# x + h made on VectorE from x with two factors per row, in place of a sum on GpSimd

## The reference, cut to what matters

```
h       = layernorm(x)                       # per row: (x - mean) * rstd
normed  = rmsnorm(h) * norm_w
h_tilde = softmax(normed q k ...) @ [normed; context]
alpha   = sigmoid(h @ gate_w.T + gate_b)
x2      = x + (1 - alpha) * h + alpha * h_tilde
        = (x + h) + alpha * (h_tilde - h)
out     = x2 + experts(layernorm(x2))
```

## Time and profile before

| What | Value |
|---|---|
| median of 3 runs | 297.89 us |
| profiled execution, its own time | 297.96 us |
| its span, first to last instruction | 296.2 us |
| attention, pairs 0 to 7 | about 16 to 88 us of the span |
| PE busy | 264.8 us (89%) |
| DVE busy | 228.5 us (77%) |
| ACT busy | 176.5 us (60%) |
| POOL busy | 158.9 us (54%) |
| mean granted TensorE clock | 0.968 |

### The profile page before, as it was taken

How to read it: one execution, slowest core, us unless ns; L and a number is a source line. 1 busy time by engine, 2 the same in 40 slices (tenths; PEclk the granted TensorE clock), 3 DMA queues, 4 the chain that set the end, 5 groups by cost and what they waited for, 6 DMA issues and landing times.

```text
span 296.2 us, 5382 instructions
## 1 busy us (share of the span) xinstructions
PE 264.8 (89%) x1677; PEld 234.0 (79%) x1677; DVE 228.5 (77%) x534; ACT 176.5 (60%) x338; POOL 158.9 (54%) x150
## 2 busy tenths in 40 slices
PE   6559999998826999999999999999999999999960
PEld 2449879896722798999999898999999999989960
DVE  3698999999881499797797787797887887966341
ACT  2437699786633667648557666657566666745410
POOL 3446845566456741466566565646645645416605
PEclk9999999999985999999999999999999999999976
DMA  6995237454352674544644543554445441201201
GB/s 206 208 364 144 71 107 212 142 161 138 114 184 82 216 256 139 144 138 158 196 137 126 176 173 124 160 163 164 143 133 197 144 140 48 71 2 63 63 11 64
DMA packets 29137, 42.06 MB, mean 142 GB/s; under 512 B 5249, under 2 KB 22859, under 8 KB 28992
## 3 DMA queue, kind: packets, MB, share of 16 engines
q1 hardware_dynamic: 24512, 29.61, 32.6%
q0 software_dynamic: 4608, 12.24, 13.1%
HBM read 33.93 MB, written 8.45 MB: 143 GB/s over the span
## 4 chain that ended last, share of the span: by engine, by line
PE 70%; DVE 8%; issue 8%; POOL 5%; DMA 4%; ACT 2%; DVEq 0%; ACTq 0%; POOLq 0%
PE bank L1060 18%; PE bank L1061 18%; PE bank L1062 18%; PE bank L1132 4%; PE bank L1101 3%; POOL out_dram L507 2%; PE bank L1147 2%; POOL x_all L501 1%; PE bank L1168 1%; PE bank L1172 1%; PE bank L1169 1%; DVE hn_cnat L721 1%; PE bank L1121 1%; DVE setup_or_probs L816 1%; DMA x_all<-token_rows,idx_all 1%
## 5 line engine op out<-in xcount | busy, mean ns | idle before, releaser
L663 ACT ACTIVATE keysT<-bank,biasT 128x512 f32<-128x512 f32 (+1 forms) x65 | 43.9, 675 | 65.2 <-PE bank L1062 56.1
L507 POOL DMA_INDIRECT out_dram<-h,sidx x32 | 38.4, 1200 | 46.6 <-DVE h L950 39.3
L501 POOL DMA_INDIRECT x_all<-out_dram,idx_all x32 | 38.7, 1211 | 23.8 <-DMA out_dram<-h,sidx 16.2
L1060 PE MATMUL bank<-x_hi,w_hi 128*128 128x512 f32 (+1 forms) x114 | 45.2, 396 | 0.0
L1061 PE MATMUL bank<-x_lo,w_hi 128*128 128x512 f32 (+1 forms) x114 | 44.5, 390 | 0.0
L1062 PE MATMUL bank<-x_hi,w_lo 128*128 128x512 f32 (+1 forms) x114 | 44.0, 386 | 0.0
L497 POOL DMA_INDIRECT x_all<-token_rows,idx_all x28 | 27.4, 980 | 22.1 <-DVE factor L1006 15.4
L958 DVE SCALAR_TENSOR_TENSOR junk<-idx_rows,idx_f,normed 128x512 bf16<-128x512 bf16 (+1 forms) x32 | 38.9, 1215 | 0.0
L989 DVE TENSOR_TENSOR w_lo<-w_raw,w_hi 128x512 fp32r<-128x512 f32 x56 | 38.3, 684 | 0.1
L1062 PE MATMUL bank<-w_hi,g_lo 128*128 128x256 f32 x128 | 36.2, 283 | 0.0
L1060 PE MATMUL bank<-w_hi,g_hi 128*128 128x256 f32 x128 | 36.1, 282 | 0.1
(11 more groups left out here) (141 smaller groups left out, 711.9 us busy)
## 6 DMA issues: line engine op xcount, KB each, us to landing
w_raw<-in_L_ffn_W_dram SPq DMA_DIRECT2D x32, 512.0 KB, 3.7
hn_cnat<-in_ctx_dram SPq DMA_DIRECT2D x8, 256.0 KB, 2.7
idx_rows<-in_L_ffn_top_idx_dram SPq DMA_DIRECT2D x8, 256.0 KB, 4.0
out_dram<-x SPq DMA_DIRECT2D x8, 256.0 KB, 2.4
token_rows<-xn SPq DMA_DIRECT2D x7, 256.0 KB, 2.2
x_all<-in_x_dram SPq DMA_DIRECT2D x2, 768.0 KB, 11.2
hn_cnat<-in_L_ffn_b_dram SPq DMA_DIRECT2D x1, 1024.0 KB, 6.7
x_all<-in_x_dram SPq DMA_DIRECT2D x2, 256.0 KB, 3.7
```

Of the source, the lines that this page charges most:

```text
L501: g.indirect_dma_start(accg[:, t, :], None, flat, list_of(e, t)).then_inc(acc_in, 16)
L507: g.indirect_dma_start(flat, idx(sidx[:, t:t + 1].bitcast(U32), 0), newrow[:, t, :], None, bounds_check=N - 1, oob_is_err=False).then_inc( ...
L663: a.activation(g32[:, f % NG, c], ps_up[j % 2][:, c], ACT.Gelu_apprx_tanh, bias=bias)
L1060: t_.matmul(dst, lhs_hi, rhs_hi, start=first, stop=False)
```

## The change

POOL no longer computes x + h. DVE makes two factors per row once for all batches (in three groups, behind the statistics they come from) and then, in each pair, two `tensor_scalar` instructions of 256 numbers a row that multiply x by the one and add the other. They stand behind `h_rows` and ahead of the reciprocal and `shift`. `h_rows` no longer waits for POOL's reading of h, and `residual` waits for DVE's own instructions instead of POOL's.

```diff
+        xh_scale = sb("xh_scale", [P, NB])
+        xh_shift = sb("xh_shift", [P, NB])
...
             def attention(p, s, use):                      # POOL
-                pool.wait_ge(h_rdy, 2 * p + 2)
-                g.tensor_tensor(x_plus_h[:, s, :], x_all[:, ds(p * (2 * H), 2 * H)],
-                                h[:, s, :, :].rearrange("p b h -> p (b h)"), ALU.add).then_inc(xh_rdy, 1)
...
             def h_rows(p, s, reused=True):                 # DVE
                 if reused:
-                    dve.wait_ge(xh_rdy, p - 1)
                     dve.wait_ge(diff_rdy, 2 * p - 2)
...
+            def xh_factors(b0, b1_):
+
+                v.tensor_scalar(xh_scale[:, b0:b1_], pow_out[:, 0, b0:b1_], 1.0, None, ALU.add).then_inc(x_steps, 1)
+                v.tensor_tensor(xh_shift[:, b0:b1_], neg_mean[:, b0:b1_], pow_out[:, 0, b0:b1_], ALU.mult)\
+                    .then_inc(x_steps, 1)
+                steps[0] += 2
+
+            def x_plus_h_rows(p, s):
+
+                for b in range(2):
+                    v.tensor_scalar(x_plus_h[:, s, b * H:(b + 1) * H], x_all[:, ds((2 * p + b) * H, H)],
+                                    xh_scale[:, ds(2 * p + b, 1)], xh_shift[:, ds(2 * p + b, 1)],
+                                    ALU.mult, ALU.add).then_inc(xh_rdy, 1)
...
             def residual(p, s, use):
                 dve.wait_ge(mix_rdy, p + 1)
-                dve.wait_ge(xh_rdy, p + 1)
+                dve.wait_ge(xh_rdy, 2 * p + 2)
...
             def attention(p, s, use):                      # DVE
...
                     x_rms(10, NB, 5)
+                    xh_factors(10, NB)
...
                 if is_first(p):
                     x_variances(10, NB)
+                    xh_factors(0, 4)
+                    dve.wait_ge(x_steps, steps[0])
                 else:
                     aggr2(p - 1, 1 - s)
                     if not is_last(p):
                         h_rows(p + 1, 1 - s)
+                x_plus_h_rows(p, s)
                 dve.wait_ge(exp_rdy, 2 * p + 2)
                 v.reciprocal(rinv[:, :], rsum[:, :]).then_inc(ri_rdy, 1)
                 if is_first(p):
                     x_rms(4, 10, 4)
+                    xh_factors(4, 10)
                     dve.wait_ge(x_steps, steps[0])
...
-            dve.wait_ge(xh_rdy, NPAIR)
+            dve.wait_ge(xh_rdy, 2 * NPAIR)
```

## The result

The kernel after takes 305.43 us (305.39 to 307.19) against 297.76 us for the kernel before in the same runs: a ratio of 1.0267, with a 95% interval of 1.0224 to 1.0311. That is +7.7 us, where +10.0 us (308.0 us) was forecast; the time lies in the range and the mechanism is the one called the double block. The profiled execution took 305.46 us.

What follows compares the result with a forecast made beforehand. A loop through DVE, ACT and PE bounds the attention: 6.50 us from `shift`'s end to the next `h_rows`. 8.7 + 0.9 + 0.5 + 0 - 0.1 = +10.0 us, 297.96 + 10.0 = 308.0 us; range 300.0 to 309.5 us.

Steps and rivals of the forecast that it cites:

- the double block: Attention pairs 1 to 4: POOL's `w_lo` and `normed` each hold up DVE ahead of `shift`; 308.0 us, chance 0.50.
- (a): POOL drops its sum, 1.28 us a pair; `mix` and `residual` fall to 0.69 us, 0.7 to 0.9 us a pair.
- (b): Two new DVE rows a pair, ahead of the reciprocal and `shift`: 0.335 us each, 0.67 us for two.
- (c): New rows and `shift` wait for POOL's `w_lo` and `normed`; `shift` ends 3.75 or 3.85 us after H, start of `h_rows`.
- (d): Five attention beats, each from one `h_rows` start to the next: 50.07 against 41.37 us, +8.7 us.
- the single block: Rival in the attention beats: `w_lo` comes after the second row, only `shift` waits; beat 9.05 us, 303.2 us, chance 0.17.
- (e): Last pairs: pair 6 +0.9 us, `shift` waiting for `w_lo`; pair 7 +0.5 us, no POOL work beside it.
- (f): Pair 0: small instructions, a wait and two rows, 1.1 to 1.4 us, covered by DVE's waits: 0, other end +0.3 us.
- (g): Start: L721's second row is free 0.9 us earlier, but a load of x comes late next: -0.1 us.
- (h): Dropped or moved waits of `h_rows` and `residual`: cost 0; the experts move as a block.
- the sliding of `w_lo` behind `shift`: Rival in the attention: rows and `shift` finish before POOL's `w_lo` and `normed`; beat 8.0 us, 297.3 us, chance 0.15.
- No block for the new rows: Rival in the attention: POOL does not hold up the rows, `shift` waits for `w_lo` alone; 300.5 us, chance 0.13.

Runs made afterwards that it cites:

- two waits: Kernel after with POOL's `expert0_lo` waiting for `shift` and `normed_rows` waiting for `residual` of the same pair: ratio 0.9972 to the kernel before.
- The first of these waits: POOL's `expert0_lo` waits for `shift` of the same pair, here added to the kernel before: 299.08 us, ratio 1.0031.
- The kernel with the last rows early: Kernel after with the new rows ahead of `hnT_low`, those of pairs 6 and 7 one pair earlier: 299.31 us, ratio 1.0027.

## Why the prediction was right, and where its sizes were off

**(a) POOL's sum goes: right.** `mix` and `residual` fell to 0.69 us, and in the first four beats this brought nothing, as the loop closes on ACT's side (DVE idles 0.62 to 1.36 us ahead of `hnT_low`). Without any sum the gain is 0.5%.

**(b) Two rows of 0.335 us: right,** 408 ns each, 0.73 us the pair. The reason given, no double rate since 408 ns are the statistic's 410, is wrong: the likeness was chance, 288 ns with immediate numbers and 0.12 us for the factors. The rule of the Trainium skill, "VectorE: DVE Perf Modes", Mode 2×_2P, is borne out by the 0.13 us for 256 numbers more; the result that I drew from it, both rows through ahead of `w_lo`, came with immediate numbers.

**(c) The double block: right in place and order, 0.3 us too long.** `shift` ended at H + 3.44, 3.51, 3.52, 3.51 us, against 3.75 and 3.85. The mis-sized term is what a row still takes after POOL's instruction ends: I took its whole 0.3 us, measured are 0.15 us (46.92 to 47.07). `normed` did not wait for it but started at 46.88 us and was done at H + 3.50 instead of 3.7, and `shift` ended 0.01 to 0.02 us behind `normed` in pairs 2 to 4.

**(d) The beats: +6.9 us measured, +8.7 forecast.** The first three, 9.94, 10.01 and 10.01 us, are (c) + 6.50. The fourth, 10.91 us, has 0.9 us that no part of the prediction had: the clock, below. The fifth, 7.42 us against 8.77, is where the double block failed. `shift` ended at H + 2.52 there, since `w_lo` came at 76.75 us (H + 1.10), behind the second row: the single block, 1.3 us less. The margin of 0.09 us named in the rival decided for the double block in pairs 2 to 4 and against it in pair 5. From `shift` (78.17 us) to the next H (83.07 us) are 4.90 us, as forecast (4.92). The 0.9 us of the clock hide as much of the overestimate: that the sum came as near as it did is to that extent luck.

**(e) Pairs 6 and 7: +1.4 us forecast and measured,** 8.45 us from H of pair 6 to the last difference (83.07 to 91.52) against 7.09 us before, but not by the forecast way in pair 6. `w_lo` waited there for ACT until 84.67 us, and `shift` was through at H + 1.51. What came later was PE's values product and logits: DVE waited 0.22 and 0.45 us for them. The parts were 0.6 us up to the rows of pair 7 (0.9 forecast) and 0.7 us behind them (0.5), so that the sum agreed is in part luck.

**(f), (g) Pair 0 and the start: H of pair 1 is 0.18 us later,** 0 and -0.1 forecast. The third load was what came late next, as said: the two instructions of L720 take 1.66 us (2.61 before), DVE is ready at 15.1 us and waits 0.36 us for it, until 15.47 us. That is 0.69 us earlier than before. The lead was lost at PE's gate product, for which DVE waits 0.75 us until 21.88 us: from 20 to 22 us the granted clock is 0.50. In the second profiled execution of the kernel after the clock stays at 1.00 there and the statistics start at 16.32 us, and H of pair 1 is 34.78 us again. Pair 0 behind that added nothing, as forecast: DVE's values stand 1.18 us later (27.76 against 26.58 us), `mix` 0.24 us.

**(h) The experts moved as a block: nearly.** At DVE's last difference of the attention the kernel is 8.46 us behind, at the experts' first three-pass product 9.45 us (98.49 against 107.94 us), at PE's last one 7.55 us (288.70 against 296.25 us), over the span 7.5 us. About half of the first 1.0 us is clock: the first product of the experts starts 8.95 us later (97.57 against 106.52 us), and from there to the three-pass product the kernel after takes 1.42 us at the lower level (granted clock 0.50 from 106 to 108 us), the kernel before 0.92 us. A part of the return behind it is clock too: the kernel before has a stretch at the lower level late in the experts that the profiled execution of the kernel after has not (each line by the stretch, with PE's busy time and granted clock; first before, then after):

```profile
284.00:288.00 4.00, 3.46 (x17) 0.57 0.02 4
```

```profile
291.50:296.50 5.00, 3.06 (x24) 1.00 0.02 3
```

How the rest of the 1.9 us divides I did not settle; it was argued from two profiles, not tried.

**The rivals.** The single block came true in pair 5 and with immediate numbers; the sliding of `w_lo` behind `shift` in pair 6 and, put there by a wait, in all pairs, with 40.6 us for five beats. "No block for the new rows" is refuted by the 1375 ns and by the statistics in their place.

## What to carry to other kernels

Before work moves between VectorE and GpSimd, look for instructions of the same form that last two or three times as long as their shortest while the other engine works on large operands: here that was the sign that the engines already take turns, and a turn cost nearly a whole GpSimd instruction, however short the one that waited (0.16 us became 1.2). Price such a change by which instructions stand side by side ahead of the result that the loop waits for, not by the sums of work. When two engines take turns, a wait that keeps them apart can be worth more than the work moved: here two waits took back 2.9%, where the kernel without any sum is 0.5% faster than the kernel before. The first of these waits in the kernel before gave nothing (ratio 1.0031), since there the block only moved to `mix` and `residual`: look at what stands where the other engine's work goes.

## What the runs showed of the hardware that I had not expected

A `tensor_scalar` of 128x256 fp32 from SBUF to SBUF takes 288 ns with immediate numbers and 408 ns with two factors per row; one of 512 with factors took 0.54 us where two of 256 took 0.73. With factors or with immediates the one of 256 was held up by a GpSimd `tensor_tensor` of 128x512 (up to 1375 and 1385 ns), and a statistics instruction over the same data did not (two in 0.74 us under `w_lo`). A GpSimd `tensor_tensor` of two numbers a row did not hold up the same form: beside `rstd`, 0.88 us from 44.61 us in the kernel after, `h_rows` took its 0.73 us from 44.72 us.

The clock fell in the attention. In the fourth beat of the kernel after the granted clock is 0.84 on the mean (the stretch above); PE had waited 2.03 us for ACT's rows, then its transposes L1073 started at 70.47 us and the clock was at its lower level, 1.2 of 2.4 GHz, until 73.9 us. The stretch, and the transposes one beat earlier and in this beat:

```profile
70.40:73.80 3.40, 3.33 (x16) 0.51 0.92 158
```

```profile
60.47 0.66 PE L1073 MATMUL bank<-ident,hn_cnat 128*128 128x128 f32 x4 [1.88 <-ACT hn_cnat L594]
...
70.47 1.12 PE L1073 MATMUL bank<-ident,hn_cnat 128*128 128x128 f32 x4 [2.03 <-ACT hn_cnat L594]
```

The beats before it have the same wait (2.19, 1.87 and 1.88 us) without a fall, and the second profile of the kernel after has the fall at the same place. It made this beat 0.9 us longer than its neighbours, 10.91 against 10.01 us. DVE's four instructions more in this beat (71.19 to 71.69 us, two of them new with the change) are not the cause, since DVE waited 1.36 us for ACT's keys behind them. The kernel with the last rows early has a fall in pair 6 of its profiled execution, behind a wait of PE of 2.11 us: granted clock 0.50 from 78 to 80 us. So a longer wait on PE can cost more than itself; when it does, these runs don't say.
